# Normalising the attention probabilities on GpSimd before their transposes, in two self-attention layers of a four-layer decoder

## The reference, cut to what matters

```python
# L2a: 16 heads of 64, 4 key/value heads, rotary positions, no mask
# L3a: 16 heads of 64, causal mask
def attention(xn):                      # xn = layernorm(x), 8 batches of 256 rows
    q, k, v = heads of xn @ W           # L2a rotates q and k by position
    A = einsum('bhqd,bhkd->bhqk', q, k) * 64**-0.5
    A = softmax(A, axis=-1)             # exp(A - max) / sum
    o = einsum('bhqk,bhkd->bhqd', A, v)
    return merge_heads(o) @ Wo + bo
```

## Time and profile before

| what | value |
|---|---|
| time, median of 3 runs (lowest to highest) | 2776.68 us (2775.05 to 2780.43) |
| the profiled execution, its own time | 2782.93 us |
| its span on the core | 2781.1 us |
| PE busy over the span | 2335.9 us, 84% |
| DVE, ACT, POOL busy over the span | 56%, 49%, 26% |
| mean granted TensorE clock (1 is 2.4 GHz) | 0.921 |

### The profile page before, as it was taken

One profiled execution on the slowest core, in us unless ns is written; L12 is line 12 of the kernel. 1 busy time (PEld: TensorE's weight loads), 2 busy tenths in 40 slices (PEclk: granted clock), 3 DMA queues, 4 the chain that ended last, 5 costly groups with the idle time before them and its releaser, 6 DMA issues. The chain is left out here.

```text
span 2781.1 us, 48541 instructions
## 1 busy us (share of the span) xinstructions
PE 2335.9 (84%) x16549; PEld 1490.2 (54%) x16595; DVE 1546.6 (56%) x4593; ACT 1362.9 (49%) x3631; POOL 728.6 (26%) x1007
## 2 busy tenths in 40 slices
PE   6969998778898499953759999876969998799989
PEld 4634444745555144431646766555947776366653
DVE  4757772146666677733026666462447776677730
ACT  3736662135554266644217677431326655455542
POOL 0123212444434323102542232114421111322100
PEclk9979999979999699976779999997979999899999
DMA  2023225120000233230440000243520000332200
GB/s 78 2 77 94 86 61 177 37 76 31 25 23 16 57 101 93 65 97 15 93 85 1 2 2 1 80 90 104 162 72 2 1 2 11 99 81 82 61 18 15
DMA packets 129748, 158.29 MB, mean 57 GB/s; under 512 B 23121, under 2 KB 92122, under 8 KB 128355
## 3 DMA queue, kind: packets, MB, share of 16 engines
q1 hardware_dynamic: 117220, 143.47, 18.1%
q0 software_dynamic: 9664, 10.41, 1.8%
q10 hardware_dynamic: 2624, 1.32, 0.3%
HBM read 119.28 MB, written 36.56 MB: 56 GB/s over the span
## 5 line engine op out<-in xcount | busy, mean ns | idle before, releaser
L542 ACT ACTIVATE L3x_p_ring<-L3x_ps_t 128x512 f32<-128x512 f32 x256 | 142.0, 598 | 114.6 <-PE L3x_ps_t L622 113.8
L438 DVE CUSTOM_DVE_ANT_0 L3x_ps_s<-L3x_ps_s,L3x_mask_q 128x512 f32<-128x512 f32 x256 | 169.9, 718 | 38.1 <-PE L3x_ps_s L601 37.0
L542 ACT ACTIVATE L1x_p_ring<-L1x_ps_t 128x512 f32<-128x512 f32 x256 | 140.5, 619 | 87.7 <-PE L1x_ps_t L620 87.7
L441 DVE TENSOR_REDUCE L0x_mx<-L0x_ps_s 128x2 f32<-128x1024 f32 x128 | 152.3, 1221 | 40.3 <-PE L0x_ps_s L601 39.1
L542 ACT ACTIVATE L0x_p_ring<-L0x_ps_t 128x512 f32<-128x512 f32 x256 | 140.8, 622 | 66.8 <-PE L0x_ps_t L620 66.8
L441 DVE TENSOR_REDUCE L1x_mx<-L1x_ps_s 128x2 f32<-128x1024 f32 x128 | 152.2, 1221 | 30.5 <-PE L1x_ps_s L601 29.5
L965 ACT ACTIVATE L2a_probs<-L2a_ps_s,L2a_top 128x256 f32<-128x256 f32 x256 | 117.8, 472 | 78.9 <-DVE L2a_top L915 78.9
L965 ACT ACTIVATE L3a_probs<-L3a_ps_s,L3a_top 128x128 f32<-128x128 f32 (+1 forms) x256 | 104.0, 422 | 39.3 <-DVE L3a_top L911 37.2
L620 PE MATMUL L3x_ps_t<-L3x_q_stack,L3x_k_stack 128*128 128x256 bf16 x512 | 120.6, 275 | 2.7 <-DMA L3x_q_stack<-L3x_m_rows 2.4
L622 PE MATMUL L3x_ps_t<-L3x_mask_k,const_ident_bf 128*128 128x256 bf16 x512 | 119.9, 273 | 0.0
L620 PE MATMUL L0x_ps_t<-L0x_q_stack,L0x_k_stack 128*128 128x256 bf16 x512 | 86.4, 278 | 9.3 <-DMA L0x_q_stack<-L0x_m_rows 3.8
(11 more groups left out here) (718 smaller groups left out, 6204.9 us busy)
## 6 DMA issues: line engine op xcount, KB each, us to landing
L2f_w_e<-L2f_in_w_e SPq DMA_DIRECT2D x23, 544.0 KB
L0x_k_stack<-L0x_k_dram SPq DMA_DIRECT2D x96, 96.0 KB
L1x_k_stack<-L1x_k_dram SPq DMA_DIRECT2D x96, 96.0 KB
L3x_k_stack<-L3x_k_dram SPq DMA_DIRECT2D x96, 96.0 KB
L0f_w<-L0f_in_w SPq DMA_DIRECT2D x32, 256.0 KB, 5.3
L1a_rk_wide<-L1a_rk_dram SPq DMA_DIRECT2D x8, 1024.0 KB, 4.7
L1f_w<-L1f_in_w SPq DMA_DIRECT2D x32, 256.0 KB
kept_x<-ctxT SPq DMA_DIRECT2D x24, 256.0 KB, 3.7
```

The source lines that it names most:

```text
L438: last = dve.tensor_tensor_reduce(span, span, mask_q[:, t, :], 1.0, 2 * MASKED, ALU.add, ALU.max, accum_out=mx[:, t, k:k + 1])
L441: last = dve.tensor_reduce(mx[:, :, k], s_bank(o), AX, ALU.max)
L542: act.activation(p_ring[:, u % RING, j * BANK:(j + 1) * BANK], t_bank(o), ACT.Exp, scale=scale).then_inc(out["t"].sem, 1)
```

## The change

For L2a and L3a a flag `divided` is set. With it

- GpSimd multiplies the probabilities in place by the inverse sums, one instruction for each head and query tile (four for each unit, 128 x 256 in L2a, 128 x 128 and 128 x 256 in L3a), where it made the two copies into `wide`;
- PE's transposes of a head (`turn`) wait for these multiplications instead of for `exp`, and `turn` of u-1 moves to the end of unit u, behind `values` and `outputs` of u-2;
- the tiles `wide` and `spread`, PE's two transposes and ACT's copy for `spread` are dropped;
- `outputs` on DVE becomes a plain copy of `ps_o`;
- DVE's reciprocal waits, where its place in the ring of four is used again, until the multiplications that read it are done.

```diff
-        if cfg.get("turn_early"):
-            put("turn", *divmod(u - 1, U))
         put("exp", b, part)
-        if not cfg.get("turn_early"):
+        if not divided:
             put("turn", *divmod(u - 1, U))
         if ends(u - 1):
             put("inverse", *divmod((u - 1) // GROUPS, C))
         for kind, k, off in second:
             put(kind, b + off, k)
         if ends(u - 2):
-            for kind in ("spread", "values", "outputs"):
+            for kind in ("values", "outputs") if divided else ("spread", "values", "outputs"):
                 put(kind, *divmod((u - 2) // GROUPS, C))
+        if divided:
+            put("turn", *divmod(u - 1, U))
...
-                    if kind == "inverse":
+                    if kind == "inverse" and divided:
+
+                        pool.wait_ge(inverted, b * C + k + 1)
+                        for n, c, j, slot in heads_of(b, k):
+                            for t in range(QT):
+                                row = probs[:, n % P_RING, t, 0:keys_of(t)]
+                                pool.tensor_scalar(row, row, inverse[:, slot, j, t:t + 1], None, ALU.mult).then_inc(scaled, 1)
+                    elif kind == "inverse":
...
                         dve.wait_ge(exp_done, (g + 1) * R)
+                        if divided and g >= SUM_RING:
+                            dve.wait_ge(scaled, QT * R * (g - SUM_RING + 1))
                         dve.reciprocal(inverse[:, g % SUM_RING], sums[:, g % SUM_RING]).then_inc(inverted, 1)
                     if kind == "outputs":
 
                         dve.wait_ge(pv_full, g + 1)
+                        if divided:
+                            dve.tensor_copy(oT[:, b % 2, k, :], ps_o[:, 0:S]).then_inc(o_done, 1)
+                            continue
...
-                            pe.wait_ge(exp_done, n + 1)
+                            if divided:
+                                pe.wait_ge(scaled, QT * (n + 1))
+                            else:
+                                pe.wait_ge(exp_done, n + 1)
```

More of the change, by code:

```diff
@@ L672, in attention_rows @@
     s_banks, m_banks = cfg["s_banks"], cfg["m_banks"]
-    name = cfg["name"]
+    name, divided = cfg["name"], cfg.get("divided")
     G = B * C
@@ L754, in attention_rows @@
         inverse = sb("inverse", [P, SUM_RING, R, QT])
-        wide = sb("wide", [P, 2, QT, P])
         probs = sb("probs", [P, P_RING, QT, S])
         probsT = sb("probsT", [P, T_RING, 2 * S])
-        spread = sb("spread", [P, 2, S])
+        if not divided:
+            wide = sb("wide", [P, 2, QT, P])
+            spread = sb("spread", [P, 2, S])
         oT = sb("oT", [P, 2, C, S])
@@ L770, in attention_rows @@
         s_full, top_done, exp_done = sem("s_full"), sem("top_done"), sem("exp_done")
-        inverted, widened = sem("inverted"), sem("widened")
+        inverted, widened, scaled = sem("inverted"), sem("widened"), sem("scaled")
         turn_full = sem("turn_full")
@@ L3586 @@
    slots=[([("v",0,0)],[("y",0,-2),("y",1,-2)]),([("x",0,1)],[("ln",0,2)]),([("q",0,1)],[]),([("k",0,1)],[("ln_rest",0,2)])]),
- 'L2a':dict(chunks=8,kd=64,rope=True,out_bias=True,kchunks=2,vcols=256,s_banks=3,m_banks=2,q_scale=1.0,kchunk=lambda c:c//4,
+ 'L2a':dict(chunks=8,kd=64,rope=True,divided=True,out_bias=True,kchunks=2,vcols=256,s_banks=3,m_banks=2,q_scale=1.0,kchunk=lambda c:c//4,
    vhead=lambda c,j:L2_PAIRS[c][j]//4,q_to="dve",k_to="dve",v_to="act",copies=("act","act"),
@@ L3590 @@
           ([("q",1,1)],[("y",1,-1)]),([("q",2,1)],[]),([],[("ln",0,2)]),([("q",3,1)],[("ln_rest",0,2)])]),
- 'L3a':dict(chunks=8,kd=64,causal=True,out_bias=True,kchunks=8,vcols=1024,s_banks=3,m_banks=2,q_scale=-64**-0.5,kchunk=lambda c:c,
+ 'L3a':dict(chunks=8,kd=64,causal=True,divided=True,out_bias=True,kchunks=8,vcols=1024,s_banks=3,m_banks=2,q_scale=-64**-0.5,kchunk=lambda c:c,
    vhead=lambda c,j:2*c+j,q_to="act",k_to="dve",v_to="dve",copies=("act","dve"),
```

## The result

The changed kernel takes **3250.36 us** (median of 6 runs, 3249.07 to 3253.32) against 2776.21 us before (6 runs): 1.170 times the time, 95% interval 1.1687 to 1.1717, that is +474 us. The forecast was +128 us: right in sign and place, far too small in size.

A forecast was written before the change was run, and what follows sets the result against it. PE was taken as the bound before the change, a loop through PE, DVE and GpSimd in L2a after it. L2a +107, L3a +6 and clock +15 sum to +128 on 2776.7: 2905 us, range 2868 to 3000.

The forecast's parts named there:

- The loop: L2a: PE, DVE and GpSimd wait in a circle once a unit; trips 7.69 or 4.68 us, +107 us.
- PE stays the bound: Rival: multiplications are ready before PE wants them, only dropped transposes count; 2737 us, chance 0.05.
- the rotation is hidden: Rival: in L2a the rotation does not lengthen the trip, 105 us and the low clock fall away; 2785 us, chance 0.04.
- the dropped transposes: PE: two fewer transposes a unit, 0.32 us, 20 us of work in each of L2a and L3a.
- The multiplication: GpSimd in L2a: 0.42 us for each 128 x 256 multiplication, four in a row 1.50 us of each trip.
- The line through the clamp and the copy: GpSimd: one-input operations of 613 ns (512 columns) and 292 ns (128) give 399 ns for 256; 0.42 us taken.
- The bound from above: Rival: GpSimd's multiplication by a column costs as much as a two-input operation, 724 ns; 3024 us, chance 0.15.
- The clock: L2a: PE's clock falls in idle gaps, 1.4 us more in half of 21 units; +15 us, bounds 0 and 29.
- The rival of the low clock: Clock stays low through L2a: 1.4 us more in every unit, batch 68.4 us, time 3013 us; chance 0.08.
- The half turn: End of each L2a trip on PE: the second head's half of the turn takes 0.44 us.
- L3a's term: L3a: loop eats PE's gain, batch 35.9 against 35.92 us; first and last batches cost more, +6 us.
- The range: Whole kernel: 2868 to 3000 us for 8 in 10, taking in a good part of the dear multiplication.

The follow-up runs named there:

- e14: Changed kernel with the two-step multiplication and 6 filler matmuls on PE ahead of the first half turn of L2a's units with a rotation: 2968.73 us.
- e11: Changed kernel with turn, values and outputs one unit later, more probs slots and the two-step multiplication: 2764.62 us, 0.9955 times the kernel before.
- e3: Changed kernel with the reciprocal and multiplications moved ahead of the rotation (in L3a, of the copy of v): 3058.51 us.
- e8: Changed kernel with GpSimd's multiplication replaced by a two-step minimum and maximum with constants, normalisation left out: 2945.23 us.
- e1: Changed kernel with GpSimd multiplying by a constant instead of the column of inverse sums, normalisation left out: 3198.77 us.
- e9: Changed kernel with a second step, a multiplication by 1.0, added to GpSimd's multiplication by the column: 2984.97 us.
- e2: Changed kernel with filler matmuls (10 and 6) ahead of PE's waits for the multiplications in L2a: 3182.57 us.

## Why the prediction was right and wrong

**The loop: right.** The chain from scores to scores was the one forecast, link by link: up to GpSimd's multiplication 5.61 forecast, 5.63 in e14. PE's waits before the transposes, units with a rotation longer than those without, and GpSimd's busy share as a poor guide all came as described. The last two rivals fell (PE stays the bound; the rotation is hidden): their conditions hold only in e11 and in e3, where the order was changed to make them hold. And where PE is the bound, in e11, the time is 2764.6 and not the 2737 that the rival gave, since it counted 0.32 us a unit for the dropped transposes.

**The multiplication: the step that failed.** "Four: 3 x 0.36 + 0.42 = 1.50" measured 3.62. The line through the clamp and the copy is right for what it was drawn through: e8, a clamp of 256 columns, took 0.40, and gave 2945 us, within the forecast's own bounds of 2868 to 2950 though not at 2905. What failed was to take an instruction of one step as cheaper than, or equal to, one of two. The bound from above (0.72, the two-input addition) was taken for the dearest case, and it was not. The trace of before held a row of the right kind that I passed over, a one-step multiplication by a constant, 16 columns wide:

```profile
L2820 POOL TENSOR_SCALAR L1a_limit<-L1a_limit 128x16 f32<-128x16 f32 x8 | 2.0, 252 | 0.7
```

Through e1's two widths a line gives 529 - 112 x 2.49 = 250 ns at 16 columns, as that row has it; e8's line gives 293 - 112 x 0.83 = 200. One width tells no slope, so the row could not have given 0.92, but 252 ns for 16 columns beside 292 for 128 was a sign that the line did not fit this form. Price of the step: e9, the same order with the two-step form, is at 2984.97, so **265 of the 345 us** between forecast and result hang on it, what it does to the clock included.

The Trainium skill has a rule for this (GPSIMD Engine Reference, sections 3 and 4.1): a one-input operation runs at about line rate, 128 numbers a cycle at 1.2 GHz. The two-step forms agree with it in their slope alone (0.83 ns a column, beside 190 to 270 ns that every instruction costs in e8 and e9); the one-step form does not, it takes three times as long a column (2.5 ns). Here the measurement decides.

**The clock: right in kind, too rare.** "Scores and half a turn cost about 1.4 us more" measured 0.95 + 0.49 = 1.44. But it was counted for half of 21 units; with the dear multiplication PE waits in every unit (in the batch shown, 0.7 to 1.1 us ahead of the second half of the turn and up to 4.2 ahead of the first), and it ran at 0.69 to 0.71 in all batches of L2a but the last (0.78). There the loop also has a link that the forecast did not have: PE's projection, for which DVE's products wait. The unit before the trip above:

```profile
1624.65 2.07 PE L1030 MATMUL L2a_ps_m<-L2a_xT,kept_a 128*128 128x256 f32 x4
...
1626.76 1.29 DVE L904 TENSOR_TENSOR L2a_tilted<-L2a_ps_m,kept_a 128x512 f32<-128x512 f32 x2 [0.72 <-PE L2a_ps_m L1030]
```

Three of this batch's five units with a rotation have this wait (0.5 to 0.7 us), and they take 11.8 to 12.1 us. e2 gets back 68 us, against the 15 that were forecast for the whole layer. It is only in part an error of its own: with the two-step form, near the forecast's price, the same order has a clock of 0.86, and e14's fillers win 16 us. The rival of the low clock had the mechanism and a batch of 68.4 at the cheap multiplication; e9 has 61.

**The half turn, the dropped transposes and L3a: mis-sized terms.** Half a turn was taken at 0.44 and is 0.56 (e14), 8 us over 64 units. The dropped transposes were taken at 0.32 us a unit, 40 us in two layers; where PE is the bound they are worth 0.06 to 0.07 (e11), about 8 us. That is most of what L3a's term missed. A batch with multiplications near my price (e8) took 37.27, not 35.9, and PE goes through its ordinary unit without a wait:

```profile
2325.29 0.93 PE L1057 MATMUL L3a_ps_s<-L3a_kT,L3a_qT 64*128 64x128 f32 x8
...
2326.15 1.99 PE L1030 MATMUL L3a_ps_m<-L3a_xT,kept_a 128*128 128x256 f32 x8
...
2328.07 0.87 PE L1091 MATMUL L3a_ps_o<-L3a_probsT,L3a_v 128*64 128x256 f32 x8
...
2328.88 0.87 PE L1072 MATMUL L3a_ps_p<-const_ident,L3a_probs 128*128 128x128 f32 x6
```

The next scores start at 2329.68, 4.39 us after these, as in e11, where the forecast had 4.14 for PE and 4.19 for the loop; units with an output projection take 5.30 instead of 5.08. The links of the loop (`max` after 0.96, 1.23, reciprocal 0.26, multiplications 1.27) came as forecast and end at 2329.01, early enough for PE. With the one-step form the loop sets the unit, at 5.97, and a batch takes 50.66.

**The remainder.** From e14 back to the forecast without its clock term (2890) are 79 us. The multiplication at 1.85 instead of 1.50 is 22 of it in L2a, the half turn 8, L3a 8 x (39.02 - 35.9) = 25. The other 24 are not assigned to links by a run; the first batch of L2a (65.99 at clock 0.84, against 57.5 for the others) and the dips of the clock in every second batch lie in them.

**The range.** It took its upper end from the forecast's terms, and the one term that no row of before showed had too near an upper bound.

## What to carry to other kernels

When an engine that looks idle is put between two steps of a full one, write out the chain from one pass of the loop to the next: its length decides, not the busy shares, and putting the consumer one pass later in the order (one more slot of a ring) won 446 us here at an unchanged price of the step. Price an instruction by a row of its very form (the engine, the operation, the number of steps, the operands) and at two widths; where none is there, the range has to reach well past the dearest neighbour. What a dropped instruction takes in the trace is not yet what a full engine gains: 0.32 us a unit became 0.06 here. A filler that keeps the clock up must be shorter than the wait that it fills, so it has to be sized anew when the wait changes.

## What the runs showed of the hardware

GpSimd's multiplication by a scalar with one step took 2.5 ns for each further column of f32 (with 128 rows), and the same instruction with a second step, a multiplication by 1.0, 0.83 ns: 922 against 481 ns for 256 columns. A scalar read from a column cost 74 ns an instruction more than a constant (922 and 848 with one step); with two steps the difference was 81 (481 and 400), but there the operations differ too. Two tensors, the second one number repeated along each row, were in between, 1.66 ns a column, and writing into another tile changed nothing. PE's scores in L2a took 2.08 us at the low level of the clock and 1.13 at the high one, and while PE waited 1.1 to 4.9 us in each unit of a batch of L2a, the mean granted clock of that batch was 0.69. The same transposes and projection took PE 0.25 us more a unit in e11's order than in the order before (2.09 against 1.84).
